# Fetching one edge tile in 128 by plain row transfers from SP instead of a GpSimd gather

## The reference

```python
w = silu(edge_scalars @ fc_w1) @ fc_w2              # weights of each edge
es, ev = h_s[edge_src], h_v[edge_src]               # gather: the source node's row for each edge
m = products of w, es, ev and edge_attr             # message of each edge
agg = segment_sum(m, edge_dst)                      # sum by destination node
out = layernorm(x + self_terms(x) + agg @ W_out)
```

## Time and profile before

| What | us |
|---|---|
| median of 3 runs | 4140.89 |
| lowest and highest of them | 4140.88, 4152.81 |
| the profiled execution's own time | 4138.21 |
| its span, first to last instruction | 4136.5 |
| POOL busy in the span | 3001.8 (73%) |
| PE busy | 3309.1 (80%) |
| ACT busy | 2897.3 (70%) |
| DVE busy | 2370.1 (57%) |
| mean granted TensorE clock | 0.987 |

### The profile page before, as it was taken

One profiled execution on the slowest core, in us unless ns is written; L12 is line 12 of the kernel. 1 busy time (PEld: TensorE's weight loads), 2 busy tenths in 40 slices (PEclk: granted clock), 3 DMA queues, 4 the chain that ended last, 5 costly groups with the idle time before them and its releaser, 6 DMA issues. The chain is left out here.

```text
span 4136.5 us, 230757 instructions
## 1 busy us (share of the span) xinstructions
PE 3309.1 (80%) x91130; PEld 2547.6 (62%) x91131; DVE 2370.1 (57%) x6475; ACT 2897.3 (70%) x12105; POOL 3001.8 (73%) x3196
## 2 busy tenths in 40 slices
PE   8888888888777777777888888888878777777777
PEld 6666666666555555555766666666656565566556
DVE  6555555555444444444556666666666666666667
ACT  6666666666666666666477777777778777777776
POOL 5777777777777777777457777777777777777771
PEclk9999999999999999999999999999999999999998
DMA  5333333333222222222244334434333333333333
GB/s 156 83 84 84 83 83 83 83 86 83 73 73 73 72 73 73 73 73 72 83 123 108 104 105 109 106 104 108 105 105 98 94 94 96 94 94 96 94 94 111
DMA packets 361345, 381.19 MB, mean 92 GB/s; under 512 B 173457, under 2 KB 282677, under 8 KB 361182
## 3 DMA queue, kind: packets, MB, share of 16 engines
q0 software_dynamic: 150048, 256.28, 24.1%
q1 hardware_dynamic: 209936, 122.14, 10.4%
q10 hardware_dynamic: 1296, 1.91, 0.2%
HBM read 356.28 MB, written 23.76 MB: 92 GB/s over the span
## 5 line engine op out<-in xcount | busy, mean ns | idle before, releaser
L552 POOL DMA_INDIRECT e_rows<-scratch_table,k_index x3126 | 2954.9, 945 | 998.8 <-issue 886.1
L581 ACT ACTIVATE e_match<-e_match,e_attr 128x40 f32<-128x40 f32 x10976 | 2476.7, 316 | 0.0
L617 PE MATMUL e_sum<-e_match,e_msg 128*32 128x40 f32 (+1 forms) x81536 | 1440.6, 215 | 677.3 <-DVE e_msg L817 342.8
L617 PEld LDWEIGHTS e_sum<-e_match,e_msg 128*32 128x32 f32 x81536 | 1295.0, 111 | 995.8 <-DVE e_msg L820 376.4
L812 DVE TENSOR_TENSOR e_msg<-e_w,e_rows 128x512 f32<-128x512 f32 x784 | 541.9, 691 | 1656.4 <-DMA e_rows<-scratch_table,k_index 1608.5
L574 ACT ACTIVATE e_hidden<-e_h 100x512 f32<-100x512 f32 (+1 forms) x784 | 384.2, 490 | 1124.4 <-PE e_h L597 1116.6
L610 PE MATMUL e_w<-k_fc,e_hidden 100*128 100x192 f32 (+1 forms) x6272 | 1030.7, 367 | 0.8 <-issue 0.8
L610 PEld LDWEIGHTS e_w<-k_fc,e_hidden 100*128 100x128 f32 (+1 forms) x6272 | 812.3, 190 | 351.0 <-issue 333.0
L597 PE MATMUL e_h<-e_inputs,k_fc 128*100 128x512 f32 (+1 forms) x1568 | 713.3, 537 | 116.4 <-issue 63.7
L815 DVE TENSOR_TENSOR e_msg<-e_w,e_rows 128x384 f32<-128x384 f32 x784 | 428.7, 547 | 0.0
L817 DVE TENSOR_TENSOR e_msg<-e_w,e_rows 128x384 f32<-128x384 f32 x784 | 428.6, 547 | 0.0
(11 more groups left out here) (131 smaller groups left out, 1021.1 us busy)
## 6 DMA issues: line engine op xcount, KB each, us to landing
e_inputs<-in_inputs SPq DMA_DIRECT2D x196, 256.0 KB
e_rows<-scratch_table,k_index POOLq DMA_INDIRECT x3126
e_attr<-in_edge_attr SPq DMA_DIRECT2D x392, 24.0 KB
e_inputs<-in_inputs SPq DMA_DIRECT2D x196, 40.0 KB
e_xb<-in_xT SPq DMA_DIRECT2D x50, 128.0 KB
scratch_yT<-m_yT SPq DMA_DIRECT2D x10, 640.0 KB, 4.5
e_xb<-scratch_yT SPq DMA_DIRECT2D x50, 128.0 KB
k_index<-in_src SPq DMA_DIRECT2D x396, 4.0 KB, 3.2
```

Source lines behind the costliest of these rows:

```text
L552: pool.indirect_dma_start(out=rows[j][:, t, :], out_offset=None, in_=table_dram, in_offset=bass.IndirectOffsetOnAxis(ap=index[k][:, c:c + ...
L581: last = nc.scalar.activation(match[j][:, t, c, :], match[j][:, t, 4, :], ACT.Copy, scale=attr[q][:, e0 + t, e:e + 1])
L617: return nc.tensor.matmul(out[32 * g:32 * g + 32, c0:c0 + n, :], m[:, f:f + 32], m5[:, which:which + n, :], start=first and opens, stop=en ...
```

## The change

In each layer the bodies from 2 to 97 are taken in 12 spans of eight (`FIRST, SPAN = 2, 8`). In the last body of each span, the last tile of group 1 is no longer gathered by POOL. SP fetches it instead. A new input `row_index` holds its 128 indices as 16 rows of eight; SP loads a span's indices into SBUF, reads eight of them into registers with one register load (`values_load_multi_w_load_instructions`) and issues eight plain transfers of one row of 640 bytes each, from the table to one partition of a new buffer `kept_rows`. One half body has room for eight rows, the first half of the span's last body for sixteen and its second half for none (`BATCHES`). When all 128 rows have landed, one transfer copies `kept_rows` into `rows[1][:, 3, :]`. A new semaphore `placed` counts each body (SP adds 16 in a body without a copy), and DVE waits for it before the messages of group 1 of every body.

SP's loop and POOL's loop now cover eight bodies each rather than two, POOL computes two register values for each group rather than nine at the top of a loop, and SP's load of `attr[q]` stands between the fourth and the fifth row of a batch.

The core of the diff:

```diff
+FIRST, SPAN = 2, 8
+SPANS = (BODIES - FIRST) // SPAN
+BATCH = 8
+BATCHES = ((1, 1),) * (SPAN - 1) + ((2, 0),)
+FETCHED_GROUP = 1
...
+            def load_row_index(span):
+                sp.dma_start(row_index[:, :], d["row_index"][:, bass.ds(span * BATCH, BATCH)]).then_inc(row_index_in, 16)
+
+            def fetch_rows(batch, between=None):
+                _, numbers = nc.values_load_multi_w_load_instructions(
+                    row_index[batch:batch + 1, :], engines=[sp.engine], min_val=0, max_val=NPAD - 1,
+                    skip_runtime_bounds_check_because="sources are node numbers")
+                for r in range(BATCH):
+                    if between and r == BATCH // 2:
+                        between()
+                    p = batch * BATCH + r
+                    sp.dma_start(kept_rows[p:p + 1, :], table_dram[bass.ds(numbers[r], 1), :]).then_inc(row_in, 16)
+
+            def place_rows(span):
+                landed, summed = 16 * P * (span + 1), GPB * (FIRST + SPAN * span + SPAN - 2) + FETCHED_GROUP + 1
...
+                sp.wait_ge(row_in, landed)
+                sp.wait_ge(sum_done, summed)
+                sp.dma_start(rows[FETCHED_GROUP][:, TPG - 1, :], kept_rows[:, :]).then_inc(placed, 16)
...
+            def fetching_body(span, position, with_base):
+                i, batch = FIRST + SPAN * span + position, sum(sum(b) for b in BATCHES[:position])
+                for q, batches in enumerate(BATCHES[position]):
+                    load_inputs(i, q, (2 * (position % 2) + q + 2) % INDEX_BUFFERS)
+                    if position == 0 and q == 0:
...
+                        sp.wait_ge(row_index_in, landed)
+                        sp.wait_ge(placed, free)
+                    for b in range(batches):
+                        fetch_rows(batch + b, (lambda: load_attr(i, q)) if b == 0 else None)
+                    batch += batches
+                    if not batches:
+                        place_rows(span)
+                        load_attr(i, q)
+                if position < SPAN - 1:
+                    sp.sem_inc(placed, 16)
...
+            def spans(first, last, with_base):
+                with sp.Fori(first, last) as span:
+                    for position in range(SPAN):
+                        fetching_body(span, position, with_base)
+                    load_row_index(span + 1)
+
+            load_row_index(0)
+            for i in range(FIRST):
+                body(i, i, True)
+            spans(0, SPANS // 2, True)
...
+                fetched = started and (position, j) == (SPAN - 1, FETCHED_GROUP)
+                tiles = range(0 if started or i else EMPTY[j], TPG - 1 if fetched else TPG)
+                for t in tiles:
...
-                    ).then_inc(gathered[j], 16)
+                    ).then_inc(gathered[j], 32 if fetched and t == tiles[-1] else 16)
...
+            with pool.Fori(0, SPANS) as span:
+                for position in range(SPAN):
                     for j in range(GPB):
-                        gather(count, summed, parity, j)
+                        gather(FIRST + SPAN * span + position, position, j)
...
+                if j == FETCHED_GROUP:
+                    dve.wait_ge(placed, 16 * i + 16)
```

More of the change, by code:

```diff
@@ L55, with fetched_tile @@
 GATHERED = 16 * TPG
+FIRST, SPAN = 2, 8
[3 more added lines that the diff above has]
+FETCHED_GROUP = 1
+assert FIRST + SPAN * SPANS == BODIES and (NT - FIRST) % SPAN == 0 and SPAN % 2 == 0
+assert BATCH * sum(sum(b) for b in BATCHES) == P
+def fetched_tile(span):
+    return ((FIRST + span * SPAN + SPAN - 1) * GPB + FETCHED_GROUP) * TPG + TPG - 1
 C_S, C_X = float(np.sin(np.pi / 8)), float(np.cos(np.pi / 8))
@@ L88, in kept_tensors @@
         w[name] = ctx.enter_context(nc.sbuf_tensor("k_" + name, shape, dt))
+    w["row_index"] = ctx.enter_context(nc.sbuf_tensor("k_row_index", [P // BATCH, BATCH], I32))
     w["index"] = [ctx.enter_context(nc.sbuf_tensor(f"k_index{k}", [P, STEP], I32)) for k in range(INDEX_BUFFERS)]
@@ L465, in edge_phase @@
         e_p = ps_misc[:, 64:112].rearrange("p (t c) -> p t c", c=6)
+        kept_rows = sb("kept_rows", [P, D])
+        row_index = w["row_index"]
         prepared, zeroed, cleared = sem("prepared"), sem("zeroed"), sem("cleared")
+        row_index_in, row_in = sem("row_index_in"), sem("row_in")
+        placed = sem("placed")
         index_in = [sem(f"index_in{k}") for k in range(INDEX_BUFFERS)]
@@ L483, in _, with load_inputs @@
         def _(sp):
-            def load(i, q, k):
+            def load_inputs(i, q, k):
                 later = not (isinstance(i, int) and i == 0)
@@ L498, in load, with load_attr @@
                 sp.dma_start(inputs[q][0:layer.kin, :], d[f"inputs{L}"][:, bass.ds((2 * i + q) * cols, cols)]).then_inc(inputs_in[q], 16)
-                if later:
+            def load_attr(i, q):
+                if not (isinstance(i, int) and i == 0):
                     sp.wait_ge(e_copied, 2 * i + q - 1)
@@ L516, in store_self @@
                 sp.dma_start(d["self1"][bass.ds(i * P, P), :], self_t[:, :]).then_inc(self_out, 16)
+            def load_row_index(span):
[11 more added lines that the diff above has]
+                landed, summed = 16 * P * (span + 1), GPB * (FIRST + SPAN * span + SPAN - 2) + FETCHED_GROUP + 1
+                sp.compute_val(landed)
+                sp.compute_val(summed)
+                sp.wait_ge(prepared, 1)
+                sp.wait_ge(row_in, landed)
+                sp.wait_ge(sum_done, summed)
+                sp.dma_start(rows[FETCHED_GROUP][:, TPG - 1, :], kept_rows[:, :]).then_inc(placed, 16)
             def body(i, parity, with_base):
                 for q in range(2):
-                    load(i, q, (2 * parity + q + 2) % INDEX_BUFFERS)
+                    load_inputs(i, q, (2 * parity + q + 2) % INDEX_BUFFERS)
+                    load_attr(i, q)
+                sp.sem_inc(placed, 16)
                 if with_base:
@@ L523, in body @@
                     store_self(i - 1)
[L524 to L528, removed]
+            def fetching_body(span, position, with_base):
[3 more added lines that the diff above has]
+                    if position == 0 and q == 0:
+                        landed, free = 16 * (span + 1), 16 * (FIRST + SPAN * span)
+                        sp.compute_val(landed)
+                        sp.compute_val(free)
+                        sp.wait_ge(prepared, 1)
+                        sp.wait_ge(row_index_in, landed)
[5 more added lines that the diff above has]
+                        place_rows(span)
+                        load_attr(i, q)
+                if position < SPAN - 1:
+                    sp.sem_inc(placed, 16)
+                if with_base:
+                    load_base(i)
+                if with_base and L == 1:
+                    store_self(i - 1)
+            def spans(first, last, with_base):
[7 more added lines that the diff above has]
+            spans(0, SPANS // 2, True)
             if L == 1:
                 store_self(NT - 1)
-            with sp.Fori(NT // 2, BODIES // 2) as pair:
-                for parity in range(2):
-                    body(2 * pair + parity, parity, False)
+            spans(SPANS // 2, SPANS, False)
+            sp.wait_ge(row_index_in, 16 * (SPANS + 1))
             for k in range(2):
@@ L540, in _, with gather @@
         def _(pool):
[L541 to L544, removed]
+            def gather(i, position, j):
+                k = 2 * (position % 2) + j // 2
+                started = not isinstance(i, int)
+                if started:
+                    count, summed = 16 * (i - position % 2), GPB * i + j - GPB + 1
+                    pool.compute_val(count)
+                    pool.compute_val(summed)
                     pool.wait_ge(prepared, 1)
                     pool.wait_ge(index_in[k], count)
[L547 to L550, removed]
+                    pool.wait_ge(sum_done, summed)
+                elif i:
+                    pool.wait_ge(sum_done, GPB * i + j - GPB + 1)
+                fetched = started and (position, j) == (SPAN - 1, FETCHED_GROUP)
+                tiles = range(0 if started or i else EMPTY[j], TPG - 1 if fetched else TPG)
+                for t in tiles:
                     c = (j % 2) * TPG + t
@@ L554, in gather @@
                         in_offset=bass.IndirectOffsetOnAxis(ap=index[k][:, c:c + 1], axis=0),
-                    ).then_inc(gathered[j], 16)
-            for parity in range(2):
+                    ).then_inc(gathered[j], 32 if fetched and t == tiles[-1] else 16)
+            for i in range(FIRST):
                 for j in range(GPB):
[L558 to L564, removed]
+                    gather(i, i, j)
+            with pool.Fori(0, SPANS) as span:
+                for position in range(SPAN):
                     for j in range(GPB):
-                        gather(count, summed, parity, j)
+                        gather(FIRST + SPAN * span + position, position, j)
```

(8 more changed lines are left out.)

## The result

The changed kernel takes 4113.4 us in the median of six runs (4110.55 to 4121.87), the kernel before 4140.89 us (six runs, 4139.96 to 4152.81). The ratio is 0.9932 (95% interval 0.9918 to 0.9946): 27.5 us or 0.7% faster. Forecast were 4112 us and 28.8 us less than before.

A forecast was written before the change was run, and what follows sets the result against it. POOL's gathers were taken as the bound, with DVE waiting for them. 4138.2 - 30.0 + 0.9 + 0.3 = 4109.4 us; as the median stood 2.7 us above that execution, 4112 was given, range 4107 to 4127.

The forecast's parts named there:

- The bound: Edge phases: POOL runs back to back, one gather each 1.249 us, and DVE waits for it; 24 gathers less save 30.0 us.
- a changed pace: Sign against the forecast: POOL's gathers in both stretches no longer 1.249 us apart.
- POOL's loop: Register work moved into every group of POOL's loop is hidden by the running gather: 0 us, bound above 230.
- SP's price: SP's queue: 0.52 us a row, far end 1.6; 0.98 us a load of eight registers, far end 7.8.
- the forecast's 118.6 us a span: SP's own transfers 35.2, rows 66.6, register loads 15.7, copy and index load 1.1: 75% of a 158.6 us span.
- The half with sixteen rows: First half of a span's last body takes SP 11.9 us, so the second starts 1.9 us late; copy just in time.
- What lateness costs: SP's 1.9 us of lateness in a span's last body is regained in three groups of 32: taken as 0.
- The argument from body 50: Layer 1, about body 50: late inputs stalled PE 6.91 us, POOL lost 0.3 us, and 43 us caught it up.
- SP becomes the bound: Rival: SP's 128 transfers a span outlast POOL, from 0.83 us a row; 4634 us at 1.0 a row; chance 0.08.
- The code of POOL's loop: Rival: POOL's longer loop stalls at its 24 jumps for code fetches, 36 to 59 us, 4148 to 4171; chance 0.10.
- The sum: 4138.2 - 30.0 + 0.9 + 0.3 = 4109.4 us for the profiled execution; median given as 4112.
- the terms of 0.9 and 0.3 us: 0.9: extra `row_index` load ahead of both layers' first inputs; 0.3: at most, others catching up after the last span.

The follow-up runs named there:

- the first profile: Profiled execution of the changed kernel in its first six runs, the slowest of them: 4121.87 us.
- The second profile of the same program: The changed kernel run again unaltered, beside its three parts: 4111.19 us, 0.9929 of the kernel before; profiled execution 4112.96 us.
- The long loop alone: Against the kernel before, only POOL's loop of eight bodies with two register values a group; POOL gathers all tiles: 4139.88 us, 0.9999.
- The fetch alone: Against the changed kernel, SP fetches and copies the rows to a spare tensor and POOL gathers every tile: 4139.58 us, 1.000 of the kernel before.
- one tile in six: Against the changed kernel, constants alone: one tile fetched in every six bodies, 32 gathers less: 4100.85 us, 0.9905 of the kernel before.
- one in four: Against the changed kernel, one tile fetched in every four bodies, 24 spans a layer: 4617.4 us, 1.1151.

## Why the prediction was right, point by point

**The bound.** POOL sets the pace: right. Each gather left out is paid back at about the 1.25 us of its pitch (24 give 31.8 us, 1.33 each, with nothing in their place; 32 give 39.6, 1.24 each, with SP's part), and work on another engine is free until that engine is full. One sign named as "wrong" did show, a changed pace: 1.253 us in the first profile. The second profile of the same program has 1.250, so the change isn't the cause.

**POOL's loop.** Taken as 0: right. The long loop alone is 0.9999 (0.9989 to 1.0008).

**SP's price.** Here the prediction was off, to the safe side. A row costs 0.41 us, not 0.52: the nearest row, a transfer to one partition with a fixed address, took 0.36 us to issue, the row from a register's address takes 0.228. A load of eight registers takes 0.76 us, 0.8 with its gap, not 0.98. The 0.98 was PE's whole gap before a sum; the old trace does show a register load by itself, PE's of one value (L654), at 0.30 us. The figure in the Trainium skill (Runtime: NRT & Kernel Launch, Instruction fetch mechanics), 200 ns a register, would be 1.6 us; the trace has 95 ns a register, and the measurement decides. The jump, up to 4.2 us, was in no term of the forecast's 118.6 us a span. With it SP needs 35.2 + 128 x 0.41 + 16 x 0.8 + 1.1 + 4.2 = 106 us at most, an estimate from these prices. No error here reached the forecast time, since SP has room by either sum.

**The half with sixteen rows.** Forecast to end 1.9 us late: it ended at 863.87, 9.9 us after it began at 853.93, so about on time. The copy was issued 1.4 us into the second half in place of 4.6. The forecast had let it wait 3.2 us for the last row; but it went 1.7 us after the last row's issue, and SP's wait for rows is 0.3 us in the whole run. DVE never waited for the copy: it starts the products of that group 7.9 us after the copy's issue, released by a gather.

```profile
873.39 0.69 DVE L889 TENSOR_TENSOR e_msg<-e_w,e_rows 128x512 f32<-128x512 f32 x1 [2.20 <-DMA e_rows<-scratch_table,k_index]
```

**What lateness costs.** The argument from body 50 held in kind and not in size: the same stall of PE for the inputs comes there again. It is 6.26 us, and POOL's gap after it is 1.36 us in place of 0.58, so 1.1 us are lost where the forecast read 0.3 off a stall of 6.91. Why a shorter stall costs more isn't shown. It happens once, in layer 1; the halves of a span's last body show no such loss, since no gap of POOL from 500 to 2000 us is over 0.3 us.

```profile
3090.66 1.22 PE L672 MATMUL e_h<-e_inputs,k_fc 128*128 128x256 f32 x2 [6.26 <-DMA e_inputs<-in_inputs]
```

```profile
3097.90 0.94 POOL L631 DMA_INDIRECT e_rows<-scratch_table,k_index  x1 [1.36 <-PE e_sum L692]
```

Not forecast was ACT's 86.6 us of waiting for `attr`, which now comes behind four rows. By its waits before, ACT had 1116.6 us of idle time for the hidden layer; that has gone down to 990.9, so the new wait has eaten slack, not time. The fetch alone shows it directly, with 88.5 us of this wait and the time of the kernel before.

**The rivals.** That SP becomes the bound was the right danger at the wrong distance: the forecast put its threshold at 0.83 us a row with one tile in eight bodies. At the real price one tile in six still fits, and one in four costs 477 us. The code of POOL's loop doesn't reload. SP's does: it takes 158 packets of q14 more, and a jump takes up to 4.2 us. A pass of SP has 128 row transfers with two register instructions each, 384 instructions for the rows alone; a pass of POOL has 127 gathers and the waits of 32 groups. The rule of the Trainium skill (Runtime: NRT & Kernel Launch, Instruction fetch mechanics), that a taken branch out of the code held waits for a fetch, agrees with the trace for SP. For POOL it did not come into play, which fits its shorter pass.

**The sum.** -30.0 + 0.9 + 0.3 = -28.8 us was forecast, -27.5 and -28.8 us measured in the two sets of runs (4140.89 to 4113.4, 4140.02 to 4111.19). The agreement to a tenth in the second set is luck: the interval of that ratio is 7 us to either side. No run resolves the terms of 0.9 and 0.3 us. SP's part, forecast at 0.9, is 0 by itself and 3.0 us as the difference of two medians.

## What to carry to other kernels

Find the engine that waits for nothing, count its instructions, and price what is taken off it by its own pitch; busy shares would have named PE here. What the receiving engine can take is a budget per period: add up its issue prices, and its own transfers and jumps, and stop short of full, since beyond it each us is paid on every span. A few us of lateness inside such a period are nearly free as long as the buffers ahead of the bound are deep enough, and the place in the old trace where an input once came late shows roughly how deep they are: a stall of 6 to 7 us cost 0.3 us there and 1.1 in the changed kernel.

## What the runs showed of the hardware

- A transfer of one row of 640 bytes with its address in a register takes SP 228 ns to issue, and the next one starts 0.41 us after it. The index load over 128 partitions takes 0.37 us to issue, the copy of 128 rows within SBUF 0.53. Eight registers are loaded from SBUF in 0.76 us.
- GpSimd's pace differs by up to 0.3% between executions of one program (948 and 946 ns a gather), 7.7 us or more than a quarter of this change. The profiled execution was the slow one here; its span alone would have put the gain at 16 us.
- SP's loop, with 128 row transfers and their register work in a pass, is fetched again on each pass (6.0 to 6.6 packets of 8 KB), at up to 4.2 us a jump; POOL's loop, with 127 gathers and their waits, is not.
